# A routed feed-forward on one core: who weighs the last 29 slot tiles, and how the last four tiles' rows come home

## The reference

```python
x = L0_attn_embeddings                                  # (8, 512, 128) float32
x = layernorm(x + attention(x, W_Q, W_K, W_V))          # causal softmax attention, one head, per batch
x = layernorm(x + ffn(x))

def ffn(x):                                             # 8 experts, 128 -> 512 -> 128, each token takes 2 of them
    logits = (x @ gate_w + gate_b) / 0.9
    keep the two largest, gate_probs = softmax over these two
    h = gelu(x @ w1[e] + b1[e]);  expert_out = h @ w2[e] + b2[e]
    out = sum over e of gate_probs[e] * expert_out[e]
    return (out - mean(out)) / sqrt(var(out) + 1e-5) * ln_g + ln_b
```

## Time and profile before

| what | value |
|---|---|
| device time, median of 3 runs | 257.54 us (256.94 to 259.61) |
| the profiled execution's own time | 257.17 us |
| its span, first to last instruction | 255.4 us |
| TensorE, VectorE, ScalarE, GpSimd busy | 229.6, 173.4, 179.3, 144.3 us |
| mean granted TensorE clock | 0.970 of 2.4 GHz |

### The profile page before, as it was taken

One profiled execution on the slowest core, in us unless ns is written; L12 is line 12 of the kernel. 1 busy time (PEld: TensorE's weight loads), 2 busy tenths in 40 slices (PEclk: granted clock), 3 DMA queues, 4 the chain that ended last, 5 costly groups with the idle time before them and its releaser, 6 DMA issues.

```text
span 255.4 us, 7300 instructions
## 1 busy us (share of the span) xinstructions
PE 229.6 (90%) x1874; PEld 209.0 (82%) x1875; DVE 173.4 (68%) x958; ACT 179.3 (70%) x527; POOL 144.3 (57%) x165
## 2 busy tenths in 40 slices
PE   6988998999999799999999999999999999999100
PEld 3466876788787689999999999999999999999100
DVE  0146576787888888558953333366488999989884
ACT  3365857778675889977886555555555996599953
POOL 8400007357777777777877777775544545546500
PEclk9999999999999999999999999999999999999855
DMA  5999303023131545523328797868789686913275
GB/s 143 250 332 332 105 3 93 31 74 97 53 95 53 137 134 120 144 68 107 95 75 254 204 355 241 221 183 246 228 267 356 186 232 180 320 47 114 92 220 151
DMA packets 45105, 42.38 MB, mean 166 GB/s; under 512 B 5488, under 2 KB 34080, under 8 KB 45072
## 3 DMA queue, kind: packets, MB, share of 16 engines
q1 hardware_dynamic: 40224, 32.84, 45.2%
q0 software_dynamic: 4320, 8.92, 10.0%
q10 hardware_dynamic: 528, 0.26, 0.3%
HBM read 27.89 MB, written 12.01 MB: 156 GB/s over the span
## 4 chain that ended last, share of the span: by engine, by line
PE 78%; DVE 10%; ACT 5%; DVEq 2%; issue 2%; DMA 1%; ACTq 0%; SPq 0%
PE bank L595 26%; PE bank L584 25%; PE bank L435 6%; PE bank L462 4%; PE bank L502 3%; PE bank L421 3%; PE bank L483 2%; ACT rows L668 2%; PE bank L450 2%; ACT probs L676 2%; PE bank L426 2%; PE bank L592 2%; PE bank L416 1%; DMA wk<-in_L_attn_W_K_dram 1%; DVE sum_stats L1139 1%
## 5 line engine op out<-in xcount | busy, mean ns | idle before, releaser
L749 ACT ACTIVATE h<-bank,b_cols 128x128 f32<-128x128 f32 x284 | 81.6, 385 | 37.4 <-PE bank L584 37.0
L1340 POOL DMA_INDIRECT returned<-x,slot_back x71 | 71.3, 1004 | 43.0 <-DVE x L1120 33.2
L1335 POOL DMA_INDIRECT slots<-rows,slot_of x64 | 65.0, 1016 | 53.0 <-DVE rows L984 34.4
L595 PE MATMUL bank<-w_all,h 128*128 x568 | 78.5, 282 | 0.0
L584 PE MATMUL bank<-slot_xT,w_now 128*128 128x128 f32 x568 | 75.2, 275 | 0.1
L595 PEld LDWEIGHTS bank<-w_all,h 128*128 128x128 f32 x568 | 69.0, 192 | 0.8
L584 PEld LDWEIGHTS bank<-slot_xT,w_now 128*128 128x128 f32 x568 | 69.1, 192 | 0.3 <-DVE slot_xT L883 0.3
L881 DVE CAST slot_back<-slot_x 128x1 uint32<-128x1 f32 x71 | 10.4, 147 | 37.9 <-PE bank L584 37.8
L838 DVE TENSOR_REDUCE negmax<-bank 128x1 f32<-128x128 f32 (+3 forms) x32 | 14.7, 484 | 16.0 <-PE bank L436 15.8
L462 PEld LDWEIGHTS bank<-v,probsT 128*128 128x128 f32 x160 | 19.7, 192 | 5.7 <-issue 3.8
L1120 DVE TENSOR_SCALAR x<-bank,slot_gate 128x128 f32<-128x128 f32 x71 | 24.0, 341 | 0.2 <-PE bank L595 0.2
(11 more groups left out here) (155 smaller groups left out, 305.4 us busy)
## 6 DMA issues: line engine op xcount, KB each, us to landing
w_now<-in_L_ffn_w_dram SPq DMA_DIRECT2D x47, 256.0 KB, 3.6
slot_x<-slots SPq DMA_DIRECT2D x71, 65.0 KB
w_all<-in_L_ffn_w_dram SPq DMA_DIRECT2D x16, 256.0 KB, 5.9
pair<-returned SPq DMA_DIRECT2D x14, 256.0 KB, 3.2
rows<-rows SPq DMA_DIRECT2D x8, 256.0 KB, 3.0
x<-n_L_attn_embeddings_dram SPq DMA_DIRECT2D x7, 256.0 KB, 3.9
returned<-x,slot_back POOLq DMA_INDIRECT x71, 3.4
slots<-rows,slot_of POOLq DMA_INDIRECT x64, 2.3
```

What stands on the lines that cost most here:

```text
L595: m = nc.tensor.matmul(o, h[:, s % RING, c * P:(c + 1) * P], w2_c, start=False, stop=(c == FC - 1))
L749: m = nc.scalar.activation(h[:, s % RING, cols], bank_[:, cols], ACT.Gelu, bias=b1_cols[:, c:][:, bass.ds(first, 1)])
L1335: g_.indirect_dma_start(slots, bass.IndirectOffsetOnAxis(ap=slot_of[:, b, c:c + 1], axis=0), rows[:, k, b * TB + t, :], None).then_inc(dis ...
L1340: g_.indirect_dma_start(returned, bass.IndirectOffsetOnAxis(ap=slot_back[:, j:j + 1], axis=0), y[:, j % Y_RING, :], None).then_inc(y_retur ...
```

## The change

- **Weighing.** From tile 42 on (`WEIGHED_BY_ACT`), 29 tiles, ScalarE does `weigh`, behind `gelu` in the same body. It waits for `step_done`, for the ring entry, and for VectorE's copy of tile j + 7, which reads the same PSUM bank (`slotT_ready`).
- **Batches 2 and 3** are handled as the others (`centre`, `rescale`); ScalarE's part of them in the loop goes.
- **Roots.** ScalarE's second root in the loop (body 65) goes. Batches 4 and 5 get their first inverse root by nine small VectorE instructions (`root_link`: Newton steps on an integer guess).
- **Last four tiles** (67 to 70, `ENDING` = 67). GpSimd no longer scatters them. VectorE builds from the tile's home rows a 128x256 matrix of zeros and ones (`perm`, one instruction, and `far`, a 128x1 one before it) inside `copy_slots`; TensorE, behind all contractions, multiplies y by it (`gather`, eight products into two banks), and VectorE adds the two banks to batch 8's tiles. SP loads batch 8 together with batch 7, and early on it writes zeros to the rows of `returned` that nothing scatters to (`blanked`).
- **Outputs.** ScalarE scales batches 0 to 3 (16 tiles) only behind its last `weigh`, between the roots; GpSimd scales batches 4 and 5 (8 tiles of 128x128). The store of batches 0 to 3 is cut in two halves. SP's order of stores stays.

```diff
+    ENDING = WHOLE[-2]
...
+        WEIGHED_BY_ACT = FINAL_AT - LAG
+        ROOT_AT = 52
...
 # SP
+            for k in range(TOPK):
+                last_rows = returned[k * N + (B - 1) * S:k * N + B * S, :].rearrange("(p t) d -> p t d", p=P)
+                sp.dma_start(last_rows[:, HALF:TB, :], empty[:, 0:HALF, 0:D]).then_inc(blanked, 16)
...
             load_pair(B - 1)
-            wait_whole(4)
             load_pair(B)
...
-            sp.wait_ge(res_ready, EARLY // 2)
-            sp.dma_start(out_p[:, 0:EARLY, :], pair[:, 1, 0:EARLY, :]).then_inc(stored, 16)
+            for first in (0, EARLY // 2):
+                sp.wait_ge(res_ready, first + EARLY // 2)
+                half = slice(first, first + EARLY // 2)
+                sp.dma_start(out_p[:, half, :], pair[:, 1, half, :]).then_inc(stored, 16)
...
 # TensorE
+            def gather(k):
+                pe.wait_ge(y_ready, ENDING + k + 1)
+                pe.wait_ge(perm_ready, k + 1)
+                for t in range(HALF):
+                    m = nc.tensor.matmul(home_psum[t], perm[:, k, t * P:(t + 1) * P], y[:, (ENDING + k) % Y_RING, :],
+                                         start=(k == 0), stop=(k == LAG - 1))
+                if k == LAG - 1:
+                    m.then_inc(gathered, 1)
...
+            for k in range(LAG):
+                gather(k)
...
 # ScalarE
+            def weigh(j):
+                act.wait_ge(step_done, j + LAG + 1)
+                if j + LAG + AHEAD < J:
+                    act.wait_ge(slotT_ready, j + LAG + AHEAD + 1)
+                act.wait_ge(y_returned[j % Y_RING], 16 * (j // Y_RING))
+                nc.scalar.activation(y[:, j % Y_RING, :], psY(j % UNROLL), ACT.Copy,
+                                     scale=slot_gate[:, j % (2 * UNROLL):j % (2 * UNROLL) + 1]).then_inc(y_ready, 1)
...
+                        if j - LAG >= WEIGHED_BY_ACT:
+                            weigh(j - LAG)
+                        if j == ROOT_AT:
+                            take_root(0)
...
+            weigh(J - 4)
+            take_root(1)
+            for j in range(J - 3, J):
+                weigh(j)
             take_root(2)
...
+            act.wait_ge(scaled, 2)
+            normalise(0, 7, res_ready)
             take_root(3)
...
+            normalise(7, 2, res_ready)
             take_root(4)
+            normalise(9, 5, res_ready)
             take_root(5)
+            normalise(14, 2, res_ready)
             take_root(6)
...
 # VectorE
+                ending = isinstance(j, int) and j >= ENDING
+                if ending:
+                    at = slot_x[:, s % UNROLL, BACK:ROW]
+                    vec.tensor_scalar(far[:, j - ENDING:j - ENDING + 1], at, float(N), -float(N), ALU.is_ge, ALU.mult)
                 vec.tensor_copy(slot_xT[:, s % RING, :], psT_of(j, s)).then_inc(slotT_ready, 1)
+                if ending:
+                    dve.drain()
+                    vec.tensor_scalar(perm[:, j - ENDING, :], home[:], far[:, j - ENDING:j - ENDING + 1], at,
+                                      ALU.subtract, ALU.is_equal).then_inc(perm_ready, 1)
...
-            FINAL += [(what, b, cost) for b in (2, 3) for what, cost in PLAIN]
+            FINAL += [("centre", 2, 5), ("centre", 3, 5)]
+            FINAL += [(what, 2, cost) for what, cost in FUSED[1:]]
             FINAL += [(what, b, cost) for b in (4, 5) for what, cost in HEAD]
-            FINAL += [("centre", 4, 5), ("centre", 5, 5), ("root", 1, 3)]
+            LINKS_FROM = len(FINAL)
+            FINAL += [("centre", 4, 5), ("centre", 5, 5)]
+            FINAL += [(what, 3, cost) for what, cost in FUSED[1:]]
+            FINAL += [("link", 4, 1)] * 4
             FINAL += [(what, b, cost) for b in (4, 5) for what, cost in FUSED[1:]]
...
+                    if b == 8:
+                        dve.drain()
+                        dve.wait_ge(gathered, 1)
+                        for t, home_sum in zip(tiles_of(b), home_psum):
+                            vec.tensor_tensor(pair[:, 0, t, :], pair[:, 0, t, :], home_sum, ALU.add)
...
 # GpSimd
-            for j in range(RETURNS_AHEAD, J):
+            for j in range(RETURNS_AHEAD, ENDING):
                 give_back(j)
+            pool.wait_ge(scaled, 2)
+            for b in (4, 5):
+                for k in tiles_of(b):
+                    m = g_.tensor_scalar(pair[:, 1, k, :], pair[:, 0, k, :], sum_rstd[:, k:k + 1], sum_shift[:, k:k + 1],
+                                         ALU.mult, ALU.add)
+                m.then_inc(late_ready[b], 1)
```

88 lines of the change are left out of this document (37 added, 51 removed).

## The result

The changed kernel took 262.13 us (median of 4 runs, 261.14 to 263.09), the kernel before on the same chip 258.58 us (4 runs, 256.94 to 259.99). The ratio is 1.015, 95% interval 1.011 to 1.020: slower, with a median 1.6 us over the forecast and inside its range. The profiled execution took 261.14 us, its span is 258.3 us (before 257.17 and 255.4).

A forecast was written before the change was run, and what follows sets the result against it. TensorE was taken to bound the kernel to its last contraction at 237.1 us, VectorE behind it. Span 255.4 + 1.2 + 0.7 + 0.15 + 0.2 + 1.1 = 258.75, plus 1.8, gave 260.5 us; range 257.4 to 262.8.

The forecast's parts named there:

- TensorE's loop unchanged, VectorE late at the end: Loop: TensorE sets the pace up to the last contraction, still near 237 us; VectorE decides when batch 5 is done.
- VectorE idles in bodies 57 to 60 and before batches 4 and 5: Late loop, a sign of being right: VectorE waits before bodies 57 to 60 and before `add` of batches 4 and 5.
- `add` of batch 6 1.2 us later: End of VectorE's loop work: this `add` starts at 238.6 us, against 237.41 before.
- the 224.1 of the sum: VectorE's start of body 65 in us; 14.5 us of copies, matrices, units and links follow up to `add` of batch 6.
- PSUM additions and reciprocal, 0.85: VectorE behind `add` of batch 6: two PSUM bank additions 0.7 us, a reciprocal over 24 tiles instead of 8 0.15.
- GpSimd's eight instructions, 1.1: Tail: GpSimd's scalings of batches 4 and 5, 2.3 us in all, hold VectorE up by 1.1 us.
- The middle of the bounds: VectorE's delay beside GpSimd's eight instructions: bounds 0 and 2.3 us, 0.29 for each; 1.1 taken.
- no meeting on the port: Rival, tail: VectorE loses nothing beside GpSimd, the forecast without the 1.1, 259.4 us; chance 0.25.
- the last store: End of the span: 1024 KB with batches 4 and 5 stand before the last three stores; 0.2 us, 0 to 1.0.
- the time beyond the span: Time outside the profiled span, added to the span of 258.75 us: 1.8 us.
- The last four tiles: Loop's end: `perm` costs VectorE 0.5 us four times, 2.0 (1.6 to 3.2); the gather on TensorE is covered by 8 us.
- keeps up: Rival: VectorE back at TensorE's pace by body 60, `add` of batch 6 at 236.8, time 257.5 us; chance 0.15.

The follow-up runs named there:

- ng_stores: The changed kernel with the last four tiles scattered as before and SP storing tiles 8 to 15 behind batches 4 and 5; 257.69 us, ratio 1.001.
- no_perm: The changed kernel without VectorE's eight instructions building the 0/1 matrices; TensorE multiplies with the identity, so last rows reach wrong tokens; 258.63 us, ratio 1.003.
- again: The changed kernel run and profiled once more, nothing altered; 261.83 us, ratio 1.013 to the kernel before.
- weigh_only: The kernel before with only ScalarE's weighing from tile 42 on added; 262.10 us, ratio 1.013.
- best_gather: The changed kernel, gather kept, with VectorE's list and ScalarE's roots of before, batches 2 and 3 scaled by ScalarE in the loop; 261.73 us, ratio 1.013.
- best_scatter: The changed kernel with VectorE's list and ScalarE's roots of before, and the last four tiles scattered instead of gathered; 260.01 us, ratio 1.008.
- order7: The changed kernel with batch 3's units ahead of `add` of batch 4 in VectorE's list and budget 7 from body 54 on; 260.07 us, ratio 1.008.
- pool_early: The changed kernel with GpSimd's eight scalings left out of the tail and eight of the same form run at the start; 260.68 us, ratio 1.009.

## Why the prediction was right, and where its sizes were off

**TensorE's loop unchanged, VectorE late at the end: right.** No wait of TensorE in the loop, last contraction at 237.6.

**VectorE idles in bodies 57 to 60 and before batches 4 and 5: right.** 0.36 us in bodies 57, 59 and 60, 0.77 and 0.94 for rows; `weigh` taken out of bodies that TensorE paces gives nothing back. One thing it does give, which I had at nothing: the load of batch 4 is issued 1.89 us behind `expand(60)`, where before has 2.55, and the changed kernel with VectorE weighing 3.67. ng_stores shows it whole: without the gather the split ends at 1.001.

**`add` of batch 6 1.2 us later: 1.35 measured.** Body 65 starts at 224.65, which is the 224.1 of the sum once the late loop is taken out, and from there to the `add` VectorE takes 14.63 us where the sum has 14.5. Inside it the terms are off with opposite signs. Copies and three matrices take 3.18, not 3.0; links 2.13, not 1.5 (0.3 of it the pause before the last one); `centre`, `rescale`, `stats` and `aggregate` 9.32, not 9.95. So part of this hit is luck. By no_perm the four matrices are worth 2.6 us with that pause, not 2.0.

**PSUM additions and reciprocal, 0.85: 0.67 measured** (0.56 and 0.11). With GpSimd's part the whole stretch grew by 0.64, not 1.95.

**GpSimd's eight instructions, 1.1: about 0.1 measured**, up to 0.3 in ng_stores. This is the mis-sized term. The instructions themselves took longer than the cast that I sized them by (3.45 us for eight alone, not 2.3), but VectorE hardly paid. The middle of the bounds was the wrong choice; the nearest row, the scatter that took 0.38 more beside VectorE, had GpSimd paying, and here too it paid the larger part. The rival "no meeting on the port" had the mechanism right. It gave 259.4, and the time came out above even the forecast, because of four things with no or little share in the sum: the last store (0.39, where I took 0.2), the loop's start (0.5, chance), the time beyond the span (2.2 to 2.8 us, where I took 1.8), and that the median lies 1.0 us above the profiled execution (again's profile, 1.6 us longer in span, has it in the loop's start and in rows that land later). For the time beyond the span no experiment tells the cause; it is open. So the mechanism was right, but that a term 1.0 us too large was made up for, and more, by things that I had not foreseen is luck.

**The last four tiles.** The prediction treats the gather as cheap on TensorE and covered, and it is; its price is on VectorE, as the sum had it, in the bodies that are VectorE's own. Without it the kernel is 0.4% above before, and level with it once the stores are in the other order.

**The rival "keeps up"** is not far from no_perm: with 2.6 us less on VectorE, it is at 258.63.

## What to carry to other kernels

Count the work that an engine loses and gains separately for the stretches that it paces and those in which another one does; only the first count. A transfer that is replaced by products still needs its index matrix built somewhere, and here that was the one engine with no time left. And before an engine is given new work, look for what stands in its queue in the worst two microseconds, not at its share of busy time (in weigh_only ScalarE was busy for 71% of the span, and full from 228 to 240 us).

## What the runs showed of the hardware

**TensorE's clock in the first part.** In best_gather and best_scatter the loop started 2.1 us late. The stretch 40 to 50 us of best_gather and of order7 (columns: stretch, its length, busy time and count, granted clock, DMA share, GB/s):

```profile
40.00:50.00 10.00, 8.67 (x54) 0.83 0.24 73
```

```profile
40.00:50.00 10.00, 8.68 (x65) 1.00 0.23 73
```

TensorE's timeline has the same two products of 512 columns at 2.00 us in best_gather and 1.13 in order7:

```profile
46.26 2.00 PE L431 MATMUL bank<-xT,mqk 128*128 128x512 f32 x2
```

```profile
45.90 1.13 PE L431 MATMUL bank<-xT,mqk 128*128 128x512 f32 x2
```

A mean of 0.83 over 10 us is 1.2 GHz in place of 2.4 for some 3.4 us. It comes after a wait of 0.95 us before 44.03 and costs 1.7 us: the products behind it start at 50.13, in order7 at 48.09, of which 0.37 was there before. order7 has that wait too and keeps its clock. In weigh_only and pool_early TensorE is slow at 9.8 us (eight 128x128 products in 2.05 us instead of 1.13); the view gives the granted clock as 1.00 there, so only the products' times show it. In after the granted clock falls to 0.50 in 88 to 90 us, but that costs nothing in the end: it is 0.53 us behind before in front of it (83.35 against 82.82) and 0.52 at `expand(60)`. The same low clock can cost 1.7 us or nothing, by where it falls.

The 29 executions of the kernel before in the last set fall in two groups, 19 from 256.9 to 258.1 us and 10 from 258.9 to 261.1. What sets them apart isn't shown: no execution of the upper group was profiled, and its mean granted clock is no lower (0.969 against 0.968).

**GpSimd beside VectorE.** Eight 128x128 instructions with two per-partition operands: 4.05 us beside VectorE, 3.45 alone; VectorE's eight two-input instructions beside them: 2.37 against 2.27. In ng_stores the same meeting cost VectorE more: `rescale` 1.31 us, with a scatter beside its start, and a 128x256 `add` 0.56 instead of 0.39.
